# Reordering the end of the first mixture and moving the last additions to VectorE in a two-layer Perceiver kernel

## The chip, the cores and the metric

One Trainium2 chip, one core. The metric is the time of one execution on the device, in microseconds. The kernel is one launch with some 15,000 instructions on TensorE (matmuls), VectorE, ScalarE, GpSimd and SyncE (which issues most DMAs).

## The reference, cut to what matters

The input x is 8 sequences of 64 tokens by 256 features (512 tokens, four tiles of 128). A context of 8 x 1601 x 256 is read by cross-attention. Six steps run, each on a layer norm of x and added to x:

```python
x = x + L0_xattn(ln(x), ctx[:, :64]...)   # causal cross-attention, 16 heads of 16
x = x + L0_attn(ln(x))                    # attention through a latent of 64
x = x + L0_ffn(ln(x))                     # first mixture: 32 experts, top 4, and one shared
x = x + L1_xattn(ln(x), ctx)              # cross-attention on all 1601 keys
x = x + L1_attn(ln(x))                    # causal attention, inner layer norm
x = x + L1_ffn(ln(x))                     # second mixture: 8 experts, top 1, gelu
```

The layer norm is (x - mean) / sqrt(var + 1e-5) for each token. In the second mixture a token goes to one expert e and gets gelu(x W1[e] + b1[e]) W2[e] + b2[e].

## The kernel before, in words

Each engine runs one instruction list, written out by hand in the order in which it is issued; each engine is strictly in order, and semaphores join them. There is no planner. The tiles of x are x[:, t, :], t = 0 to 3, 128 tokens by 256 features in float32, kept in SBUF all the time.

**The end of the first mixture.** The 33 experts (L1626 up, L1640 down) add their outputs up in PSUM. For the last expert TensorE adds the four tiles in the order 0, 1, 2, 3 (L1682). Then TensorE issues 14 filler matmuls of 128x512 (keep_clock, L1315, called at L1687), which compute nothing that is used, and waits for the first normalized tile. VectorE meanwhile adds the sums to x: tile 0 (L1101), then measures tile 0 (bn_stats L881, bn_aggr L884), adds tile 1 (L1105) and tiles 2 and 3 at once (L1107), measures tiles 1 to 3 with the same two lines, and then scales tile 0 and tiles 1 to 3 (L892, called at L1110 and L1111). GpSimd computes the reciprocal root of the variance in two instructions (L446, L447), once for tile 0 and once for tiles 1 to 3.

From the normalized tile 0, TensorE makes two transposes (L1690), ScalarE copies them (L760), TensorE multiplies by the query weights (L1352), ScalarE scales and rounds the queries to bfloat16 (L766), and VectorE computes the remainders of that rounding (L1115, L1116, L1118), GpSimd copying some of them (L522, L524). TensorE then turns the queries (L1708, 16 transposes), ScalarE and VectorE copy them (L783, L1120), and the first scores (L1726) follow. Between the query product and L1708 stand TensorE's six transposes of tiles 1 to 3 (L1797), which wait for all of them to be normalized; ScalarE copies those in L781. On VectorE, L1115 is issued behind the scaling of tiles 1 to 3.

**The end of the second mixture.** Tokens are sorted into 11 blocks of 128 slots. Each block j goes through up (L1352), gelu (L866), down (L1948), and VectorE adds the bias into y_f (L1301). SyncE stores the first ten blocks to scratch_y in HBM in three DMAs (L378). Block 10 is not stored: TensorE sends it back to its tokens by a product with a one-hot matrix (L1971), one product for each tile of x, into PSUM banks. Once all three stores have landed, GpSimd issues four indirect DMAs (L558) that gather each token's row from scratch_y into y_back, tile by tile, and then adds each gathered tile to x (L564). VectorE adds the product of L1971 to that (L1308), tile by tile, and SyncE writes each tile to the output (L411).

Of the kernel before, what the change touches and what calls it, by code (L numbers as in the profile page):

```python
# [9 lines left out]
ALU = mybir.AluOpType  # L10
# [6 lines left out]
TT = TOK // P  # L17
# [21 lines left out]
NBLK = E1 + MORE  # L39
# [19 lines left out]
def build(nc, a, out, scratch_x, scratch_y, scratch_g):  # L59
    with ExitStack() as ctx:  # L60
        def sb(name, shape, dt=F32):
            return ctx.enter_context(nc.sbuf_tensor(name, shape, dt))

        def sem(name):
            return ctx.enter_context(nc.semaphore(name))
# [10 lines left out]
        x = sb("x", [P, TT, D])  # L76
        xn = sb("xn", [P, TT, D])
# [30 lines left out]
        def r2(n, dt=F32):  # L108
            at = used[0]
            used[0] += n  # L110
            assert used[0] <= 15344
            ap = R2[:, at:at + n]
            return ap if dt == F32 else ap.bitcast(dt)
# [77 lines left out]
        y_back = r2(TT * D).rearrange("p (t n) -> p t n", t=TT)  # L191
        ON_PE = (0, 1, NBLK - 1)
        oh = {j: r2(TT * P).rearrange("p (t s) -> p t s", t=TT) for j in ON_PE}
# [4 lines left out]
        def bank(i, n=512):  # L198
            return ps[:, i, 0:n]
# [9 lines left out]
        def w(key, at, n):  # L209
            o = W_COLS[key] + at  # L210
            return lambda c, lo=0, k=n: wall[:, c, o + lo:o + lo + k]
# [12 lines left out]
        def sems(prefix, names):  # L224
            return {n: sem(f"{prefix}_{n}") for n in names.split()}
# [59 lines left out]
        mq = sems("mq", "neg ln xt_ps xt q_ps qhi qf qs qdup qt_ps qt qt_b a_ps a_max nm row_ps row s_ps exp pv o o_ps y y_ps yt out_ps x")  # L285
        m0 = sems("m0", "x_hi x_lo log_ps sig mask pos_ps gate gt_ps gt sel up_a up_b silu t g r hi mid lo down end x gates_out")
        gb_in = [sem(f"gb_in{i}") for i in range(4)]
        w0_in = [sem(f"w0_in{i}") for i in range(4)]
        m1 = sems("m1", "zero zeroed log_ps mask count_ps pos_ps slot blocks oh sent h_ps act y_ps y added oht_ps oht fin out xg_ps xgt")
        w1_in = [sem(f"w1_in{i}") for i in range(WSLOTS)]  # L290
        w2_in = [sem(f"w2_in{i}") for i in range(WSLOTS)]
        bias_in = sem("bias_in")
# [2 lines left out]
        back = [sem(f"back{t}") for t in range(TT)]  # L295
# [120 lines left out]
        def _(pool):  # L416
# [125 lines left out]
            for k in range(4):  # L542
                t = 2 + k % 2
# [8 lines left out]
            for t in range(TT):  # L552
                pool.indirect_dma_start(
                    out=scratch_x[:, :], out_offset=bass.IndirectOffsetOnAxis(ap=f_si[:, t:t + 1], axis=0),
                    in_=xn[:, t, :], in_offset=None).then_inc(m1["sent"], 16)
            pool.wait_ge(stored, 16 * 3)
            for t in range(TT):
                pool.indirect_dma_start(  # L558
                    out=y_back[:, t, :], out_offset=None,
                    in_=scratch_y[:, :], in_offset=bass.IndirectOffsetOnAxis(ap=f_si[:, t:t + 1], axis=0)  # L560
                ).then_inc(back[t], 16)
            for t in range(TT):
                pool.wait_ge(back[t], 16)
                pool.tensor_tensor(x[:, t, :], x[:, t, :], y_back[:, t, :], ALU.add).then_inc(m1["added"], 1)  # L564


        @block.scalar
        def _(act):
# [303 lines left out]
        def _(dve):  # L872
            def lk(ins):
                link(dve, dve_chain, ins)
# [3 lines left out]
            def measure(src, lo_=0, hi_=TT):  # L878

                for t in range(lo_, hi_):  # L880
                    ins = dve.bn_stats(stats[:, t, :], src[:, t, :])  # L881
                lk(ins)
                for t in range(lo_, hi_):
                    ins = dve.bn_aggr(mv[:, t, :], stats[:, t, :])  # L884
                variances[0] += 1
                ins.then_inc(var_ready, 1)
                return variances[0]

            def scale(src, dst, done, n, lo_=0, hi_=TT):
                dve.wait_ge(rstd_ready, n)  # L890
                for t in range(lo_, hi_):
                    ins = dve.tensor_scalar(dst[:, t, :], src[:, t, :], mv[:, t, 0:1], rstd[:, t, :], ALU.subtract, ALU.mult)  # L892
                    if done is not None:
                        ins.then_inc(done, 1)
                if done is None:
                    lk(ins)
# [206 lines left out]
            first = measure(x, 0, 1)  # L1103
            dve.wait_ge(m0["end"], 2)
            dve.tensor_tensor(x[:, 1, :], sum0(1), x[:, 1, :], ALU.add).then_inc(m0["x"], 1)  # L1105
            dve.wait_ge(m0["end"], 3)
            dve.tensor_tensor(x[:, 2:4, :], bank(4).rearrange("p (t n) -> p t n", t=2), x[:, 2:4, :], ALU.add).then_inc(m0["x"], 2)  # L1107
            dve.wait_ge(m0["x"], TT)
            rest = measure(x, 1, TT)
            scale(x, xn, mq["ln"], first, 0, 1)  # L1110
            scale(x, xn, mq["ln"], rest, 1, TT)  # L1111
            Qg = Qs[:, 0:H, :].rearrange("p a (g d) -> p a g d", d=HD)
            q_ps = bank(7, D).rearrange("p (h d) -> p h d", h=H)
# [171 lines left out]
            def block_turned(j):  # L1285
                dve.wait_ge(m1["xg_ps"], j + 1)
                if j >= 2:
                    dve.wait_ge(m1["h_ps"], 2 * (j - 1))
                dve.tensor_copy(xgT[j % 2], bank(5 if j == 1 else 0, D).rearrange("p (c n) -> p c n", c=C)).then_inc(m1["xgt"], 1)  # L1289

            block_turned(0)
            block_turned(1)
            one_hot(NBLK - 1)
            dve.wait_ge(bias_in, 32)
            for j in range(NBLK):
                if j + 2 < NBLK:
                    block_turned(j + 2)
                if j == E1:
                    dve.wait_ge(more_bias_in, 32 * MORE)
                dve.wait_ge(m1["y_ps"], j + 1)  # L1300
                dve.tensor_tensor(y_f[:, j, :], bank(3 + j % 2, D), b2_s[:, j, :], ALU.add).then_inc(m1["y"], 1)  # L1301
                if j == 3:
                    dve.wait_ge(m1["oht_ps"], 1)
                    dve.tensor_copy(ohT, bank(5).rearrange("p (t s) -> p t s", t=TT)).then_inc(m1["oht"], 1)
            for t in range(TT):
                dve.wait_ge(m1["added"], t + 1)
                dve.wait_ge(m1["fin"], t + 1)
                dve.tensor_tensor(x[:, t, :], bank((0, 5, 6, 7)[t], D), x[:, t, :], ALU.add).then_inc(m1["out"], 1)  # L1308


        @block.tensor
        def _(pe):
            def keep_clock(n, at):
                for _ in range(n):
                    pe.matmul(bank(at), ident_b, mask_b, start=True, stop=True, skip_group_check=True)  # L1315
# [368 lines left out]
                    if k == 2 and t != 2:  # L1684
                        ins.then_inc(m0["end"], 1)
            wq, wo = w("1x", 0, D), w("1x", D + 32, D)
            keep_clock(14, 5)  # L1687
            pe.wait_ge(mq["ln"], 1)
            for c in range(C):
                ins = pe.transpose(ps[:, 6, c * P:(c + 1) * P], xn[:, 0, c * P:(c + 1) * P], ident)  # L1690
# [229 lines left out]
            def turn_block(j):  # L1920
                for i, (lo_, _) in enumerate(XG):
                    if j == lo_:
                        pe.wait_ge(xg_in[i], 16)
                if j >= 1:
                    pe.wait_ge(m1["xgt"], j)
                for c in range(C):
                    ins = pe.transpose(ps[:, 0, c * P:(c + 1) * P], xg[:, j, c * P:(c + 1) * P], ident)  # L1927
                ins.then_inc(m1["xg_ps"], 1)
# [115 lines left out]
```

## Time and profile before

| What | us |
|---|---|
| Median of three runs | 528.6 (528.46 to 528.76) |
| The profiled execution | 528.27 |
| Its span, first to last instruction | 526.4 |
| TensorE busy | 501.4 (95%) |
| VectorE busy | 324.5 (62%) |
| ScalarE busy | 299.7 (57%) |
| GpSimd busy | 124.3 (24%) |
| Granted TensorE clock, mean | 1.000 of full |

The span starts with the first instruction; all times below are counted from there. Busy time is summed for each engine and counts neither waits nor the issuing of DMAs. The 95% of TensorE is its busy share and includes filler matmuls. The profiled execution lies 0.33 us below the median of the runs.

### The profile page before, as it was taken

Reading aid. Unit: us, or ns where it says so; the run is one execution under the profiler, and the core shown is the slowest. Engines: PE = TensorE matmul, PEld = TensorE weight load, DVE = VectorE, ACT = ScalarE, POOL = GpSimd, SP = SyncE. Lnnn points to the kernel's source line nnn. Section 1 sums busy time; section 2 is a strip of 40 time slices with the busy share of each in tenths; the row PEclk is TensorE's granted clock in tenths of the full one; section 3 lists DMA queues with packets and bytes.
Section 4 is the critical chain, followed back from the end, with each engine's and each line's share of the span. In section 5 each row is a group of like instructions: output and inputs, shape, how many; then the busy total and the mean of one; then the engine's idle time right before and its main releaser. Section 6 shows DMA issues by size and latency. Waiting matters only on the chain.

```text
span 526.4 us, 15176 instructions
## 1 busy us (share of the span) xinstructions
PE 501.4 (95%) x6412; PEld 355.0 (67%) x6426; DVE 324.5 (62%) x672; ACT 299.7 (57%) x512; POOL 124.3 (24%) x218
## 2 busy tenths in 40 slices
PE   7999998899999999789999999999999989999996
PEld 4666676556666665455767767677567658999995
DVE  4652874666666666779899889999358674101101
ACT  2465485866656653477788877887734522233311
POOL 6124126733333333430000000000042033000005
PEclk9999999999999999999999999999999999999999
DMA  8977620135555552900000000000072002998813
GB/s 311 392 269 271 236 78 2 61 76 160 147 159 149 147 158 56 384 11 2 2 4 2 4 2 4 2 4 3 2 259 66 2 0 87 263 367 278 308 60 100
DMA packets 35346, 64.37 MB, mean 122 GB/s; under 512 B 3312, under 2 KB 25328, under 8 KB 34896
## 3 DMA queue, kind: packets, MB, share of 16 engines
q1 hardware_dynamic: 34752, 62.35, 35.9%
q8 instruction: 51, 0.84, 0.6%
q0 software_dynamic: 384, 1.05, 0.6%
q14 instruction: 15, 0.12, 0.1%
q10 hardware_dynamic: 144, 0.01, 0.0%
HBM read 59.40 MB, written 4.00 MB: 120 GB/s over the span
## 4 chain that ended last, share of the span: by engine, by line
PE 81%; DVE 7%; POOL 3%; ACT 3%; issue 2%; DMA 2%; SPq 0%; POOLq 0%; DVEq 0%; ACTq 0%
PE ps L1352 14%; PE ps L1626 10%; PE ps L1758 9%; PE ps L1726 9%; PE ps L1772 7%; PE ps L1640 7%; PE ps L1948 7%; PE ps L1471 2%; PE ps L1484 2%; PE ps L1458 2%; PE ps L1327 2%; PE ps L1435 1%; DVE region L1128 1%; DMA attn_weights<-in_wall 1%; PE ps L1377 1%
## 5 line engine op out<-in xcount | busy, mean ns | idle before, releaser
L1128 DVE TENSOR_REDUCE region<-ps 128x1 f32<-128x512 f32 x192 | 124.2, 687 | 16.2 <-PE ps L1726 16.1
L816 ACT ACTIVATE region<-ps 128x1024 f32<-128x1024 f32 (+1 forms) x112 | 106.0, 963 | 20.9 <-PE ps L1758 20.4
L1726 PE MATMUL ps<-ctx_kT,region 96*32 96x512 bf16 x768 | 82.0, 383 | 1.7 <-DVE region L1128 0.8
L1758 PE MATMUL ps<-region,ctx_kT 98*32 98x512 bf16 x832 | 72.5, 381 | 0.6 <-ACT region L794 0.4
L1772 PE MATMUL ps<-region,ctx_v 128*32 128x128 f32 (+1 forms) x1664 | 70.2, 272 | 0.0
L1626 PE MATMUL ps<-region 128*128 128x512 f16 x264 | 62.9, 379 | 1.0 <-ACT ctx_kT L589 0.7
L1772 PEld LDWEIGHTS ps<-region,ctx_v 128*32 128x32 f32 (+1 forms) x1664 | 56.7, 109 | 9.3 <-issue 0.3
L866 ACT ACTIVATE region<-ps,ctx_v 128x128 f32<-128x128 f32 x88 | 25.2, 368 | 59.7 <-PE ps L1352 59.7
L507 POOL TENSOR_TENSOR region<-region 128x512 f32<-128x512 f32 x33 | 38.2, 1156 | 64.2 <-ACT region L741 62.8
L1640 PE MATMUL ps<-region 128*128 128x256 bf16 x384 | 47.2, 273 | 0.9 <-DVE region L1075 0.9
L1640 PEld LDWEIGHTS ps<-region 128*128 128x128 bf16 x384 | 37.4, 98 | 12.4 <-DVE region L1075 1.7
L1626 PEld LDWEIGHTS ps<-region 128*128 128x128 bf16 x264 | 25.2, 98 | 25.8 <-ACT ctx_kT L589 0.8
L1083 DVE SCALAR_TENSOR_TENSOR region<-ps,region 128x512 f32<-128x512 f32 x33 | 22.8, 691 | 31.5 <-PE ps L1626 31.2
L1726 PEld LDWEIGHTS ps<-ctx_kT,region 96*32 96x32 bf16 x768 | 23.3, 94 | 26.5 <-DVE region L1128 15.2
L529 POOL CAST region<-region 128x4 bf16<-128x4 f32 x15 | 2.9, 190 | 135.6 <-DVE region L1138 135.6
L1352 PEld LDWEIGHTS ps<-region 128*128 128x128 f32 x288 | 33.3, 192 | 0.3
L1352 PE MATMUL ps<-region 128*128 128x128 f32 x288 | 33.4, 274 | 0.0
L735 ACT ACTIVATE region<-region 128x512 bf16<-128x512 f32 x33 | 20.8, 630 | 22.0 <-POOL region L507 22.0
L1758 PEld LDWEIGHTS ps<-region,ctx_kT 98*32 98x32 bf16 x832 | 25.1, 96 | 7.7 <-ACT region L794 1.3
L741 ACT ACTIVATE region<-region 128x512 bf16<-128x512 f32 x33 | 20.8, 629 | 15.8 <-DVE region L1096 15.6
L1301 DVE TENSOR_TENSOR region<-ps,ctx_v 128x256 f32<-128x256 f32 x11 | 4.7, 424 | 36.9 <-PE ps L1948 36.9
L1289 DVE COPY region<-ps 128x256 f32<-128x256 f32 x11 | 4.7, 425 | 34.4 <-PE ps L1927 33.0
(234 smaller groups left out, 821.5 us busy)
## 6 DMA issues: line engine op xcount, KB each, us to landing
region<-in_w SPq DMA_DIRECT2D x15, 1024.0 KB, 8.4
region<-in_ctxT SPq DMA_DIRECT2D x8, 1601.0 KB, 8.5
region<-gates SPq DMA_DIRECT2D x30, 256.0 KB, 3.4
ctx_kT<-in_w SPq DMA_DIRECT2D x7, 1024.0 KB, 7.3
region<-in_moe SPq DMA_DIRECT2D x33, 192.0 KB, 2.4
attn_weights<-in_wall SPq DMA_DIRECT2D x1, 2152.0 KB, 22.8
slots_x<-zeros SPq DMA_DIRECT2D x1, 1408.0 KB, 10.7
attn_weights<-in_wall SPq DMA_DIRECT2D x4, 256.0 KB, 5.8
```

The lines of the kernel that those rows point to most:

```text
L507: pool.tensor_tensor(hr[n % 2], t2[n % 2], hp[n % 4][0], ALU.subtract).then_inc(m0["r"], 1)
L816: act.activation(probs[u % NP_][:, 0:512 * n_keys], ps[:, pr:pr + n_keys, :].rearrange("p b n -> p (b n)"), ACT.Exp).then_inc(mq["exp"], 1)
L866: ins = act.activation(hT[j % 2][:, k, :], ps[:, (1, 6)[j % 2] + hh, (k % 4) * P:(k % 4 + 1) * P], ACT.Gelu, bias=b1_s[:, j, k:k + 1])
L1083: ins = dve.scalar_tensor_tensor(out=dst, in0=bank(n % 2), scalar=1.0 / XS, in1=sa[n % 2], op0=ALU.mult, op1=ALU.mult)
L1128: ins = dve.tensor_reduce(mp[g % 2][:, j // 3, j % 3:j % 3 + 1], bank(4 + n % 2), AX.X, ALU.max)
L1352: ins = pe.matmul(dst, lhs(c), rhs(c), start=(c == 0), stop=(c == C - 1))
L1626: ins = pe.matmul(bank(n % 2 if part else 2 + n % 2), wn[:, c * 256 + part * 128:c * 256 + part * 128 + 128], xp[k][:, c, :], start=(c == ...
L1640: ins = pe.matmul(sum0(t), hp[n % 4][k][:, t * P:(t + 1) * P], w0[n % 4][:, 512:768], start=(n == 0 and k == 0 and t < 3), stop=False, ski ...
L1726: ins = pe.matmul(ps[32 * i:32 * i + 32, at, :], QT[0:KQ, b, h + i // 2, 32 * (i % 2):32 * (i % 2) + 32], kT[0:KQ, b, 512 * c:512 * c + 51 ...
L1758: ins = pe.matmul(ps[32 * c:32 * c + 32, 2 * (u % 2) + i, :], kT[0:KQ2, b, k * P + 32 * c:k * P + 32 * c + 32], QT[0:KQ2, b, 8 * r:8 * r + ...
L1772: ins = pe.matmul(ps[32 * c:32 * c + 32, 7, 0:P], v_ctx[0:rows_, b, k, :], probs[u % NP_][0:rows_, 512 * i + P * c:512 * i + P * (c + 1)], ...
L1948: ins = pe.matmul(bank(3 + j % 2, D), hT[j % 2][:, k, :], w2_s[j % WSLOTS][:, k, :], start=(k == 0), stop=(k == HC - 1))
```

## The change

At the end of the first mixture, VectorE scales tile 0 right after the additions, ahead of measuring tiles 1 to 3, and TensorE issues 10 filler matmuls instead of 14. At the end of the second mixture, GpSimd adds nothing any more: VectorE adds the gathered tiles 0 and 1 before the y addition of the last block, tile 2 before the first output addition, and tile 3 between the second and the third. Each of them waits for its own gather, and VectorE waits for each (lk) before its next instruction. The semaphore "added" goes.

```diff
-            for t in range(TT):
-                pool.wait_ge(back[t], 16)
-                pool.tensor_tensor(x[:, t, :], x[:, t, :], y_back[:, t, :], ALU.add).then_inc(m1["added"], 1)
...
             dve.tensor_tensor(x[:, 2:4, :], bank(4).rearrange("p (t n) -> p t n", t=2), x[:, 2:4, :], ALU.add).then_inc(m0["x"], 2)
+            scale(x, xn, mq["ln"], first, 0, 1)
             dve.wait_ge(m0["x"], TT)
             rest = measure(x, 1, TT)
-            scale(x, xn, mq["ln"], first, 0, 1)
             scale(x, xn, mq["ln"], rest, 1, TT)
...
+            def add_gathered(t):
+                dve.wait_ge(back[t], 16)
+                lk(dve.tensor_tensor(x[:, t, :], x[:, t, :], y_back[:, t, :], ALU.add))
...
+                if j == NBLK - 1:
+                    add_gathered(0)
+                    add_gathered(1)
                 dve.wait_ge(m1["y_ps"], j + 1)
                 dve.tensor_tensor(y_f[:, j, :], bank(3 + j % 2, D), b2_s[:, j, :], ALU.add).then_inc(m1["y"], 1)
...
-            for t in range(TT):
-                dve.wait_ge(m1["added"], t + 1)
+
+            def add_last(t):
                 dve.wait_ge(m1["fin"], t + 1)
                 dve.tensor_tensor(x[:, t, :], bank((0, 5, 6, 7)[t], D), x[:, t, :], ALU.add).then_inc(m1["out"], 1)
+
+            add_gathered(2)
+            add_last(0)
+            add_last(1)
+            add_gathered(3)
+            add_last(2)
+            add_last(3)
...
-            keep_clock(14, 5)
+            keep_clock(10, 5)
             pe.wait_ge(mq["ln"], 1)
```

## Rows read from the trace of the kernel before

**Rows 1.** The chain that ended last, shares of the span by engine.
```profile
PE 81%; DVE 7%; POOL 3%; ACT 3%; issue 2%; DMA 2%; SPq 0%; POOLq 0%; DVEq 0%; ACTq 0%
```

**Rows 2.** Timeline, 208.6 to 217 us: start, length, engine, line, operation, count.
```profile
208.62 2.97 PE L1315 MATMUL ps<-const_bf 128*128 128x512 bf16 x13
...
209.60 0.68 DVE L1107 TENSOR_TENSOR x<-ps,x 128x512 f32<-128x512 f32 x1
...
209.78 0.58 POOL L447 TENSOR_TENSOR ln_rstd<-ln_rstd,const_f 128x1 f32<-128x1 f32 x1
...
210.31 1.08 DVE L881 BATCH_NORM_STATS2 ln_stats<-x 128x6 f32<-128x256 f32 x3
...
211.66 0.38 DVE L892 TENSOR_SCALAR xn<-x,ln_mean_var,ln_rstd 128x256 f32<-128x256 f32 x1
...
212.09 0.44 PE L1690 MATMUL ps<-const_f,xn 128*128 128x128 f32 x2 [0.51 <-DVE xn L892]
...
213.01 1.13 PE L1352 MATMUL ps<-attn_weights,xnT 128*128 128x256 f32 x4 [0.47 <-ACT xnT L760]
213.14 1.06 DVE L892 TENSOR_SCALAR xn<-x,ln_mean_var,ln_rstd 128x256 f32<-128x256 f32 x3 [1.10 <-POOL ln_rstd L447]
214.18 0.38 ACT L766 ACTIVATE region<-ps 128x256 bf16<-128x256 f32 x1 [1.22 <-PE ps L1352]
...
214.25 0.88 PE L1797 MATMUL ps<-const_f,xn 128*128 128x128 f32 x6
...
214.59 0.42 DVE L1115 SCALAR_TENSOR_TENSOR region<-ps,region 128x256 bf16<-128x256 f32 x1 [0.39 <-ACT region L766]
...
214.91 0.85 ACT L781 ACTIVATE xnT<-ps 128x384 f32<-128x384 f32 x2
...
215.38 0.42 DVE L1118 TENSOR_TENSOR region<-region 128x256 bf16<-128x256 f32 x1
...
215.86 1.09 PE L1708 MATMUL ps<-const_bf,region 128*96 128x128 bf16 x16 [0.73 <-DVE region L1118]
...
216.54 0.59 ACT L783 ACTIVATE region<-ps 96x512 bf16<-96x512 bf16 x1 [0.78 <-PE ps L1708]
```

**Rows 3.** Timeline of TensorE in the first 9 us.
```profile
1.31 3.59 PE L1510 MATMUL ps<-yT 128*128 128x512 bf16 x8 [1.31 <-POOL yT L471]
...
8.73 0.51 PE L1435 MATMUL ps<-attn_weights,ctx64T 128*64 128x128 f32 x5 [1.17 <-DMA attn_weights<-in_wall]
```

**Rows 4.** Timeline, 516 to 524.4 us.
```profile
516.24 0.98 POOL L558 DMA_INDIRECT region<-slots_y,region  x1 [73.48 <-DMA slots_y<-region]
...
520.03 0.95 POOL L558 DMA_INDIRECT region<-slots_y,region  x1 [0.30 <-issue]
520.42 0.42 DVE L1301 TENSOR_TENSOR region<-ps,ctx_v 128x256 f32<-128x256 f32 x1 [6.60 <-PE ps L1948]
...
520.90 2.00 PE L1971 MATMUL ps<-region 128*128 128x256 f32 x8 [0.52 <-DVE region L1301]
521.00 2.77 POOL L564 TENSOR_TENSOR x<-x,region 128x256 f32<-128x256 f32 x4
...
522.23 2.37 SPq L411 DMA_DIRECT2D out<-x  x4
...
523.80 0.42 DVE L1308 TENSOR_TENSOR x<-ps,x 128x256 f32<-128x256 f32 x1 [0.25 <-POOL x L564]
```

**Rows 5.** The four gathers of L558, from issue to landing.
```profile
DMA to landing us min/median/max: 2.7/2.8/2.8
```

**Rows 6.** L1060 and L553: durations min/median/max in ns.
```profile
L1060 DVE TENSOR_TENSOR region<-const_f,region x3: 327/328/643, 102.2 to 103.9; 128x128 f32<-128x128 f32 x3
...
L553 POOL DMA_INDIRECT slots_x<-xn,region x4: 960/1005/1354, 437.5 to 441.7; - x4
```

**Rows 7.** Busy times, clock, DMA share and GB/s while one output tile moves.
```profile
523.00:523.70 0.70, 0.00 (x0) 0.00 (x0) 0.42 (x1) 0.00 (x0) 0.70 (x2) 1.00 0.55 187
```

More of the change, by code:

```diff
@@ L288, in build @@
         w0_in = [sem(f"w0_in{i}") for i in range(4)]
-        m1 = sems("m1", "zero zeroed log_ps mask count_ps pos_ps slot blocks oh sent h_ps act y_ps y added oht_ps oht fin out xg_ps xgt")
+        m1 = sems("m1", "zero zeroed log_ps mask count_ps pos_ps slot blocks oh sent h_ps act y_ps y oht_ps oht fin out xg_ps xgt")
         w1_in = [sem(f"w1_in{i}") for i in range(WSLOTS)]
```

## The prediction

> **What bounds the kernel now.** I read the chain of waits on the page first. It is TensorE for 81% of the span, with VectorE at 7% and GpSimd at 3% [rows 1]. The reader is to see that an edit on VectorE or GpSimd counts only where TensorE stands still. The change touches two such places: the hand-over from the first mixture to the cross-attention (208 to 217 us) and the last 8 us. Everything between is only shifted by what the first place gives. So I read the timeline of both places [rows 2, 4] and ask at each which arrival comes last.
>
> **Part 1, the first mixture's end.** Now the two remaining additions end at 210.28 (209.60 + 0.68, L1107). The root of tile 0 is ready at 210.36 (209.78 + 0.58, L447), while VectorE measures tiles 1 to 3 from 210.31 and scales tile 0 only at 211.66 [rows 2]. After the change the scaling waits for the later of the two, 210.36, plus 0.03 (the pause between L1107 and L881 in rows 2). So it starts at 210.39, 1.27 us earlier, and ends at 210.77 (0.38).
>
> What follows for tile 0: the transposes (L1690) at 210.83 instead of 212.09; the query product (L1352) 0.92 later, as now, at 211.75 instead of 213.01; its end at 212.88; ScalarE's copy (L766) done at 213.30 instead of 214.56 [rows 2].
>
> What follows for tiles 1 to 3: their measuring starts behind the scaling. Neighbouring VectorE instructions overlap by some 0.05 us (three of L881 take 1.08), so it starts at 210.72 instead of 210.31, 0.41 late. The aggregation, GpSimd's root and the scaling x3 follow one upon another, so the scaling x3 runs at 213.55 to 214.61 instead of 213.14 to 214.20, and the six transposes (L1797) at 214.66 instead of 214.25, done at 215.54 [rows 2].
>
> Here is the point on which this part hangs. The next step of tile 0's chain, L1115 on VectorE, needs L766, but it is queued behind the scaling of tiles 1 to 3. Now it waits for L766 (starts 214.59, VectorE idle since 214.20) [rows 2]. Afterwards L766 is ready 1.29 us before VectorE is free. L1115 starts at 214.53 to 214.62, depending on whether it overlaps the scaling or not: a change of -0.06 to +0.03, and I take -0.06, since L881 and L892 x3 in the same rows overlap. L1118 and the query transposes L1708 (215.86 now) shift by as much. Beside it, the six transposes end before 215.80; ScalarE's L781 ends at 215.76 + 0.41 = 216.17, before L783 is wanted at 216.48 [rows 2]. The 1.27 us bought for tile 0 is therefore lost in VectorE's queue, and the 0.41 us lost for the rest falls into the 0.39 us that VectorE waited there.
>
> The ten filler matmuls instead of 14 (13 recorded in 2.97, 0.23 each) end near 210.7 instead of 211.59, just before the transposes at 210.83: no delay from them, and none removed, since TensorE already stood idle before 212.09. But TensorE now has nothing from 212.88 to 214.66, 1.78 us, where it had 0.11 (213.01 + 1.13 to 214.25). That is the first rival.
>
> **Part 2, the end of the kernel.** The four gathers start from 516.24 to 520.03, 1.26 apart, and land 2.8 us after their start [rows 4, 5]: at 519.0, 520.3, 521.6 and 522.8. GpSimd adds them only once it has issued all four: 521.00 to 523.77, 0.69 each, and the last output addition (L1308) at 523.80 follows the last of these [rows 4].
>
> The price of one such addition on VectorE: no row shows it with these operands. From below 0.33 us (L1060, 128x128, two SBUF operands) [rows 6], from above 0.68 us (L1107, twice as wide) [rows 2]; I take 0.42, the 128x256 of L1118 [rows 2].
>
> - Additions 0 and 1 sit ahead of the last block's y addition (L1301, 520.42 now). Addition 0 runs at 519.03, in idle time. Addition 1 waits for 520.3 and runs until 520.72, and each is awaited before the next instruction. So the y addition starts near 520.80, 0.38 late. Queued behind it is TensorE's last group L1971 (four products in 2.00 us), which ends at 523.28 instead of 522.90.
> - Addition 2: 521.6 to 522.02. Output additions 0 and 1: 522.10 and 522.45, both products there (the first by about 522.0, the next 0.43 later).
> - Addition 3: 522.83 (landing) to 523.25. Output addition 2: about 523.33. Output addition 3: 523.67, its product there since 523.28, so 0.39 of slack. It ends at 524.09 instead of 524.22.
>
> VectorE's end moves by -0.13. With 0.33 an addition it would be -0.22, with 0.68 it would be +0.13. The last two output DMAs now follow each other by 0.34 instead of 0.68 [rows 4]. A 0.7 us stretch that holds one of them keeps the DMA engines 55% busy [rows 7], 0.39 us of full work, so the last can queue up to about 0.08 behind its neighbour. I take -0.05 for the part, with bounds -0.22 and +0.21.
>
> Do the additions disturb the gathers? GpSimd is generating gather 2 (518.8 to 519.7) during addition 0 and gather 3 (from 520.03) during addition 1. A VectorE addition of two SBUF operands took 643 ns instead of 327 beside GpSimd work, and an indirect DMA beside a VectorE burst took 1354 ns instead of 1005 [rows 6]. So both directions can cost: third rival.
>
> By the Trainium skill, page "SBUF — State Buffer", section "Who interferes with whom", a VectorE instruction with two SBUF inputs contends with a GpSimd instruction that reads SBUF, and the second to come is fully blocked; the same section infers that a tensor_tensor leaves descriptor generation alone, which would make it zero here. The trace shows the first for L1060, and nothing in it shows the second.
>
> **The sum.** 528.27 (the profiled execution; its span is 526.4) - 0.06 - 0.05 = 528.16. The runs' median, 528.6, lies 0.33 above that execution, so I forecast 528.5 us. Its own range is 528.2 to 528.8 by the bounds above (-0.28 to +0.24), widened by 0.1. About 0.2% (1.06 us) can be told from no change, so below 527.5 is faster and above 529.7 slower.
>
> **The rivals.**
> - Low clock (slower). After the 1.78 us without a matmul, the granted clock falls from 2.4 to 1.2 GHz. Against: it stayed at full over 1.17 us of nothing at 7.56 us [rows 3]. For: 1.17 us is the longest gap between matmuls in the trace before its last microseconds, so 1.78 us lies outside what it shows. Price: at the start of the kernel eight 128x512 matmuls took 3.59 us, 0.45 each, against 0.23 for the fillers [rows 2, 3]; that stretch was at least 3.6 us long, and I take 4. Four such microseconds from 215.9 on, where TensorE sets the pace, do the work of two: +2.0, 530.5 us. If it falls only for the idle time, it costs nothing. Chance 0.12.
> - The whole gain passes (faster). Tile 0's queries come 1.27 us earlier through to the first scores: 527.2 us. It would need L1115 ahead of the scaling of tiles 1 to 3 in VectorE's order, which it isn't. I leave 0.06 for this and for any other shift of the schedule over 1 us.
> - Additions and gathers disturb each other. If addition 1 is held until gather 3 is issued (520.98), the y addition is 1.05 late, L1971 ends at 523.95 and the output at 524.4: +0.18 in place of -0.13, 528.8. If instead the gathers stretch by 0.35 each (1354 - 1005), the last lands 0.7 later: 529.2. Both stay within what counts as no change. Chance 0.10.
> - The tail doesn't move since the span's end hangs on something else: 528.55, the same answer, inside the forecast.
>
> **How the numbers follow.** Forecast 0.72, clock 0.12, whole gain 0.06, disturbance 0.10. Of the forecast's share I give 0.02 to each side for what I have not seen, so faster 0.08, same 0.78, slower 0.14. The range 527.9 to 529.6 holds forecast and disturbance and leaves out the two ends, less than 2 in 10.
>
> **What would show it.** L892 for tile 0 at 210.4; the x3 scaling at 213.55; L1115 directly behind it with no wait for ScalarE; L1708 within 0.1 of 215.86; the granted clock 1.00 through 212 to 222. At the end: the y addition at 520.8, L1971 0.38 later, the last output addition at 523.7 and waiting for the gather, not for GpSimd. Wrong if L1708 moves by more than 0.3 us, if matmuls after 215 take twice their time, or if the gathers start more than 1.3 us apart.

## The result, and the profile after

| | Kernel before | Changed kernel |
|---|---|---|
| Median, 20 executions each | 528.6 us | 529.26 us |
| Range | 528.07 to 529.69 | 528.75 to 532.74 |
| Mean granted clock | 1.000 in the profiled execution | 0.990 to 0.997 in 19 executions, 1.000 in one (528.91 us) |

The ratio is 1.0018 with a 95% interval of 1.001 to 1.0025: slightly slower, where I forecast slightly faster. The time lies inside the range that I gave, but on the other side of 528.6, and the experiments below lay this to the granted clock. The profiled execution is the slowest of the 20 (532.74 us). 2.56 us of that are not the change's: the first addition of the stage, L1097 here, starts at 210.84 against 208.27, behind an unchanged first mixture. Three waits of TensorE for DMAs account for about that much: 2.46 us instead of 1.17 for the attention weights at 9.6 us, and 0.63 and 0.73 us for the experts' weights at 120.44 and 145.63, where the trace of the kernel before has no such wait of 0.5 us or more. Over the 12 profiles of the experiments, all with the same first mixture, that start lies between 208.4 and 210.0. So from here on I count within the two changed places from that addition ("from the stage's start"), and at the end from the first gather.

The share of the span by engine in the chain that ended last, for the changed kernel (compare [rows 1]):

```profile
PE 65%; issue 16%; DVE 7%; POOL 4%; DMA 4%; ACT 3%; SPq 0%; POOLq 0%; DVEq 0%; ACTq 0%
```

The timeline of the changed kernel around the end of the first mixture (start, length, engine, line, operation; it answers to [rows 2], whose lines 1315, 892, 881, 1690, 1352, 1115, 1797, 1118, 1708 are 1325, 888, 877, 1700, 1362, 1111, 1807, 1114, 1718 here):

```profile
210.84 0.43 DVE L1097 TENSOR_TENSOR x<-ps,x 128x256 f32<-128x256 f32 x1 [0.38 <-PE ps L1692]
...
210.96 2.32 PE L1325 MATMUL ps<-const_bf 128*128 128x512 bf16 x10
...
212.96 0.41 DVE L888 TENSOR_SCALAR xn<-x,ln_mean_var,ln_rstd 128x256 f32<-128x256 f32 x1
213.29 1.07 DVE L877 BATCH_NORM_STATS2 ln_stats<-x 128x6 f32<-128x256 f32 x3
...
213.42 0.44 PE L1700 MATMUL ps<-const_f,xn 128*128 128x128 f32 x2
...
214.34 1.13 PE L1362 MATMUL ps<-attn_weights,xnT 128*128 128x256 f32 x4 [0.47 <-ACT xnT L756]
...
216.04 1.11 DVE L888 TENSOR_SCALAR xn<-x,ln_mean_var,ln_rstd 128x256 f32<-128x256 f32 x3 [1.33 <-POOL ln_rstd L447]
217.07 0.41 DVE L1111 SCALAR_TENSOR_TENSOR region<-ps,region 128x256 bf16<-128x256 f32 x1
...
217.20 1.54 PE L1807 MATMUL ps<-const_f,xn 128*128 128x128 f32 x6 [1.74 <-DVE xn L888]
...
217.85 0.42 DVE L1114 TENSOR_TENSOR region<-region 128x256 bf16<-128x256 f32 x1
...
218.54 1.91 PE L1718 MATMUL ps<-const_bf,region 128*96 128x128 bf16 x16
```

Read it against [rows 2]. L1111 starts with no wait of its own, right behind the scaling x3. TensorE waits 1.74 us ahead of L1807 (the gap foreseen as 1.78). Then the same six transposes take 1.54 us instead of 0.88, and the sixteen of L1718 take 1.91 instead of 1.09. The busy times in four stretches give the reason (PE, PEld, DVE, ACT, POOL busy, then the granted clock, DMA share and GB/s):

```profile
211.00:216.30 5.30, 3.85 (x18) 1.73 (x15) 3.75 (x13) 1.15 (x3) 2.23 (x5) 1.00 0.78 252
216.40:219.80 3.40, 2.60 (x18) 2.59 (x19) 2.00 (x7) 1.15 (x3) 0.40 (x1) 0.50 1.08 382
219.80:223.20 3.40, 3.40 (x19) 1.75 (x17) 1.54 (x3) 1.45 (x2) 0.00 (x0) 0.50 1.06 372
223.20:226.60 3.40, 3.40 (x29) 1.75 (x28) 2.51 (x4) 1.32 (x4) 2.29 (x5) 1.00 1.03 377
```

The granted clock is at 0.50, that is 1.2 of 2.4 GHz, from 216.4 to 223.2 us: it fell inside the gap from 215.47 (214.34 + 1.13) to 217.20.

The end of the kernel (L1289 is the addition of a gathered tile, L1304 the y addition, L1981 the last products, L1311 the output addition; compare [rows 4]):

```profile
520.89 0.99 POOL L558 DMA_INDIRECT region<-slots_y,region  x1 [73.55 <-DMA slots_y<-region]
...
523.44 0.95 POOL L558 DMA_INDIRECT region<-slots_y,region  x1 [0.30 <-issue]
523.65 0.43 DVE L1289 TENSOR_TENSOR x<-x,region 128x256 f32<-128x256 f32 x1 [5.19 <-DMA region<-slots_y,region]
524.70 0.95 POOL L558 DMA_INDIRECT region<-slots_y,region  x1 [0.31 <-issue]
524.95 0.43 DVE L1289 TENSOR_TENSOR x<-x,region 128x256 f32<-128x256 f32 x1 [0.87 <-DMA region<-slots_y,region]
525.41 0.42 DVE L1304 TENSOR_TENSOR region<-ps,ctx_v 128x256 f32<-128x256 f32 x1
...
525.89 2.00 PE L1981 MATMUL ps<-region 128*128 128x256 f32 x8 [0.87 <-DVE region L1304]
526.20 0.43 DVE L1289 TENSOR_TENSOR x<-x,region 128x256 f32<-128x256 f32 x1 [0.36 <-DMA region<-slots_y,region]
526.70 0.79 DVE L1311 TENSOR_TENSOR x<-ps,x 128x256 f32<-128x256 f32 x2
...
527.42 0.42 DVE L1289 TENSOR_TENSOR x<-x,region 128x256 f32<-128x256 f32 x1
527.88 0.76 DVE L1311 TENSOR_TENSOR x<-ps,x 128x256 f32<-128x256 f32 x2
```

The output is complete on VectorE 7.75 us after the first gather started (528.64 - 520.89), against 7.98 before (524.22 - 516.24). On VectorE the tail is 0.23 us faster, and the y addition's 0.34 us delay (4.52 against 4.18 after the first gather) is hidden.

### The profile page after: what moved, and what is told of

Its sections match the earlier page's. It is cut to its first block, busy times and chain, and to the rows that moved or that the text cites. A ratio compares the mean times of both kernels' runs of the same rounds, so it can differ in the third digit from the quotient of the medians.

```text
span 530.9 us, 15182 instructions
## 1 busy us (share of the span) xinstructions
PE 504.6 (95%) x6422; PEld 356.3 (67%) x6422; DVE 326.2 (61%) x676; ACT 300.1 (57%) x512; POOL 121.5 (23%) x214
## 3 DMA queue, kind: packets, MB, share of 16 engines
q0 software_dynamic: 384, 1.05, 0.6%
## 4 chain that ended last, share of the span: by engine, by line
PE 65%; issue 16%; DVE 7%; POOL 4%; DMA 4%; ACT 3%; SPq 0%; POOLq 0%; DVEq 0%; ACTq 0%
PE ps L1636 9%; PE ps L1768 9%; PE ps L1736 9%; PE ps L1782 7%; PE ps L1650 7%; PE ps L1362 7%; PE ps L1494 2%; PE ps L1481 2%; PE ps L1468 2%; PE ps L1337 2%; DMA region<-in_moe 2%; PE ps L1445 1%; DVE region L1124 1%; DMA attn_weights<-in_wall 1%; PE ps L1387 1%
## 5 line engine op out<-in xcount | busy, mean ns | idle before, releaser
L1362 PEld LDWEIGHTS ps<-region 128*128 128x128 f32 x288 | 33.3, 192 | 0.3
L1362 PE MATMUL ps<-region 128*128 128x128 f32 x288 | 33.5, 274 | 0.0
L927 DVE TENSOR_REDUCE region<-ps 128x8 f32<-128x512 f32 x24 | 16.5, 689 | 14.2 <-PE ps L1468 13.9
```

What stands on the lines that cost most here:

```text
L1362: ins = pe.matmul(dst, lhs(c), rhs(c), start=(c == 0), stop=(c == C - 1))
```

## The experiments

Theory: the clock's fall in the new gap makes the change slower; without it the change is worth some -0.1 to -0.2 us. Rival: the moved additions cost it at the end. Each kernel ran 12 times, beside 35 runs of the kernel before on the same chip; three chips served the three groups. "Low" are executions whose mean granted clock was 0.997 or less, and medians are given apart for the two kinds. The kernel before's own executions are counted without a single one of 537.83 us.

| Kernel | Median us | Low | Median, full clock | Median, low | Ratio to before (95%) |
|---|---|---|---|---|---|
| *first group: before* | 528.83 | 9 of 34 | 528.48 | 529.69 | |
| after_fill14 | 529.17 | 6 of 12 | 528.00 | 529.73 | 0.9998 (0.9984 to 1.0013) |
| after_gapfill | 528.66 | 2 of 12 | 528.58 | 529.76 | 0.9992 (0.9976 to 1.0008) |
| before_fill10 | 529.94 | 9 of 12 | 528.26 | 530.08 | 1.0010 (0.9996 to 1.0025) |
| tail_only | 528.52 | 4 of 12 | 528.39 | 530.15 | 0.9997 (0.9982 to 1.0012) |
| *second group: before* | 529.35 | 13 of 35 | 528.94 | 530.02 | |
| after_again | 529.45 | 8 of 12 | 528.40 | 529.71 | 0.9998 (0.9983 to 1.0012) |
| head_only | 529.10 | 6 of 12 | 528.45 | 529.44 | 0.9998 (0.9985 to 1.0011) |
| reordered | 529.40 | 4 of 12 | 529.03 | 530.56 | 1.0005 (0.9990 to 1.0020) |
| reordered_route | 528.63 | 0 of 12 | 528.63 | | 0.9988 (0.9975 to 1.0000) |
| *third group: before* | 529.23 | 10 of 35 | 528.87 | 530.17 | |
| before_route | 528.90 | 0 of 12 | 528.90 | | 0.9995 (0.9980 to 1.0009) |
| after_route | 530.05 | 12 of 12 | | 530.05 | 1.0016 (1.0000 to 1.0033) |
| gapfill_route | 528.37 | 0 of 12 | 528.37 | | 0.9990 (0.9975 to 1.0005) |
| fill14_route | 528.21 | 0 of 12 | 528.21 | | 0.9982 (0.9967 to 0.9998) |

**First group: which part is it?**

```diff
 after_fill14 (on the changed kernel)
-            keep_clock(10, 5)
+            keep_clock(14, 5)
```

> The changed kernel with 14 fillers again instead of 10 at the end of the first mixture. Clock theory (the change is slower because TensorE's granted clock falls to half for some 3.5 us in the gap behind the first query product, and the rest of the change is worth about -0.1 us): the fillers now end near 211.6 on the scale of the kernel before, the first transposes wait for them and not for VectorE (0.8 us later than with 10), the gap behind the query product shrinks from 1.8 to about 1.0 us, the clock stays at 1.000, and the time is the kernel before's -0.1 (within 0.3). Rival, the tail (VectorE's four additions disturb gathers or hold the y addition): the clock is 1.000 and the time stays 0.6 to 1.0 us above the kernel before.

The first transposes did wait for the fillers (3.15 us from the stage's start, against 2.58 with 10), and this cost the query transposes only 0.02 us (7.50 against 7.48 in after_again). But the clock was low in 6 of 12 and the time 529.17 beside 528.83, both against my expectation. The profiled execution shows where: not at the first mixture's end, but in the routing of the second mixture, which the change doesn't touch.

```profile
431.80:435.20 3.40, 2.52 (x28) 1.63 (x28) 1.81 (x15) 1.85 (x3) 0.00 (x0) 1.00 0.00 0
435.20:438.70 3.50, 3.50 (x14) 1.53 (x11) 3.31 (x16) 0.00 (x0) 0.75 (x1) 0.51 0.02 5
```

So there are two places, and every count until then mixed them. That the kernel before had low executions as well (9 of 34) was new too: its one profile had shown 1.000 throughout.

```diff
 after_gapfill (on the changed kernel)
             queries(0)
+            keep_clock(7, 5)
             pe.wait_ge(mq["ln"], TT)
```

> The changed kernel, 10 fillers kept, and 7 more fillers of 128x512 behind the first query product (1.6 us in the 1.8 us gap). Clock theory: clock 1.000, nothing delayed since TensorE stood idle there, time the kernel before's -0.1 (within 0.3), 0.6 to 1.0 below the changed kernel. Tail rival: as slow as the changed kernel, +0.6 to +1.0.

Two low executions of 12 instead of 19 of 20. The median is 528.66, 0.17 below the kernel before's beside it, in the expected direction but within its interval. Where the two low ones fell isn't shown.

```diff
 before_fill10 (on the kernel before)
-            keep_clock(14, 5)
+            keep_clock(10, 5)
```

> The kernel before with only the fillers cut from 14 to 10; VectorE's order and the tail as before. TensorE is then idle 1.4 us ahead of the first transposes, 0.5 ahead of the query product, 0.1 and 0.7 behind it: as much in sum (2.7 us) as in the changed kernel (2.6 us), but no single gap of 1.8. If the fall of the clock hangs on the sum of idle time over these 5 us, the clock falls here too (0.997 or so) and the time is +0.4 to +1.0. If it hangs on the one long gap, the clock is 1.000 and the time is the kernel before's within 0.2.

The clock fell in 9 of 12, beside 9 of 34 for the kernel before, with VectorE's order untouched: cutting four fillers alone is enough, and no single gap of 1.74 us is needed. The longest here is 1.38 us, and the fall, at 214.8, came after it, while TensorE worked on the query product. Some of the nine may be falls in the routing, as in after_fill14; the profiled one is not. Its timeline on TensorE, and the clock from 214.9 on:

```profile
213.05 0.44 PE L1690 MATMUL ps<-const_f,xn 128*128 128x128 f32 x2 [1.38 <-DVE xn L892]
213.96 1.27 PE L1352 MATMUL ps<-attn_weights,xnT 128*128 128x256 f32 x4 [0.47 <-ACT xnT L760]
215.21 1.54 PE L1797 MATMUL ps<-const_f,xn 128*128 128x128 f32 x6
```
```profile
214.90:218.20 3.30, 3.10 (x19) 2.39 (x19) 1.55 (x5) 1.91 (x5) 0.80 (x2) 0.50 1.08 384
```

```diff
 tail_only (on the kernel before: the change's last part alone)
-                pool.tensor_tensor(x[:, t, :], x[:, t, :], y_back[:, t, :], ALU.add).then_inc(m1["added"], 1)
...
+                lk(dve.tensor_tensor(x[:, t, :], x[:, t, :], y_back[:, t, :], ALU.add))
```

> The kernel before with only the last part of the change: VectorE instead of GpSimd adds the gathered rows. Clock theory: clock 1.000, the last output addition starts at 523.65 to 523.7 instead of 523.80 and the time is -0.05 to -0.15. Tail rival: +0.6 to +1.0, with gathers further apart than 1.3 us or a y addition over 0.5 us late.

As expected and against the rival: 528.52, and 528.39 where the clock is full, beside 528.48. The gathers start 1.25 to 1.30 us apart, against 1.24 to 1.28 before. The interval still reaches +0.6 us, so it is the trace that clears the tail: VectorE ends 7.82 us after the first gather, against 7.98. With that, only the head is left.

**Second group: the change again, its head alone, and the lost 1.27 us.**

after_again is the changed kernel, unaltered.

> The changed kernel once more, unaltered, beside the three others. Clock theory: the granted clock falls in nearly every execution (mean 0.996 or 0.997) and the time is +0.4 to +1.0 on the kernel before. Rival (its first measurement was a chip's or a run's peculiarity): clock 1.000 in most executions and a time within 0.2 of the kernel before.

Inconclusive for the time: 8 of 12 low against 13 of 35, ratio 0.9998. With some 1.2 us for a low execution (next section), 67% against 37% makes +0.36, and with -0.2 for the rest of the change +0.2: less than 12 executions resolve. Its profiled execution had the full clock.

```diff
 head_only (on the kernel before)
             dve.tensor_tensor(x[:, 2:4, :], ...)
+            scale(x, xn, mq["ln"], first, 0, 1)
             dve.wait_ge(m0["x"], TT)
             rest = measure(x, 1, TT)
-            scale(x, xn, mq["ln"], first, 0, 1)
...
-            keep_clock(14, 5)
+            keep_clock(10, 5)
```

> Only the first part of the change: VectorE scales tile 0 first, 10 fillers; the tail as before. Clock theory: falls in nearly every execution, +0.5 to +1.1. Tail rival: no slower than the kernel before. Either way L1708's counterpart starts 7.48 us after the first addition of the stage when the clock is full (7.59 in the kernel before).

6 of 12 low, where nearly all were expected; the profiled one fell in the head:

```profile
212.70:216.10 3.40, 1.42 (x12) 0.90 (x11) 2.20 (x6) 1.59 (x4) 1.57 (x3) 1.00 1.10 378
216.20:219.60 3.40, 3.40 (x25) 2.24 (x23) 1.71 (x3) 1.61 (x2) 0.00 (x0) 0.50 1.05 394
```

The query transposes started 7.48 us from the stage's start, just as foretold, since the clock fell only at 7.8: 1.5 us behind the end of the 1.74 us gap, with TensorE at work since 214.72 but for a wait of 0.25. The time (529.10 beside 529.35) is a miss for the clock theory's +0.5 to +1.1.

```diff
 reordered (on after_gapfill)
 VectorE:
-            scale(x, xn, mq["ln"], rest, 1, TT)
             (L1111, L1112, L1114: remainders of tile 0's queries)
+            scale(x, xn, mq["ln"], rest, 1, TT)
 TensorE:
             keep_clock(7, 5)
+            turn_queries(0, 0, 2)
+            turn_queries(0, 1, 3)
             pe.wait_ge(mq["ln"], TT)
 (ScalarE copies the turned queries ahead of tiles 1 to 3 as well.)
```

> The changed kernel with three further edits: VectorE computes the remainders of tile 0's queries ahead of scaling tiles 1 to 3, TensorE turns tile 0's queries ahead of transposing tiles 1 to 3 (and ScalarE copies in that order), and 7 fillers stand in the gap behind the first query product. If tile 0's 1.27 us are lost in VectorE's queue, as predicted, they now come through: the query transposes start about 6.3 us after the stage's first addition instead of 7.5, the first scores 1.0 to 1.3 us earlier, and the time is 0.8 to 1.3 us below the kernel before where the clock stays full. Rival: the first scores are held by something else (tiles 1 to 3, now 1.0 us later, are wanted by the second query product), and the time is the kernel before's -0.2 to +0.2.

The query transposes came at 6.35 us from the stage's start instead of 7.48, and the first scores at 8.13 instead of 8.81. Then nothing was left of it. TensorE in reordered, and then in gapfill_route, whose head is that of after_gapfill (stage's starts 210.02 and 208.43):

```profile
217.34 0.88 PE L1810 MATMUL ps<-const_f,xn 128*128 128x128 f32 x6
218.15 0.62 PE L1736 MATMUL ps<-ctx_kT,region 96*32 96x512 bf16 x8
219.37 1.13 PE L1362 MATMUL ps<-attn_weights,xnT 128*128 128x256 f32 x4 [0.61 <-ACT xnT L781]
```
```profile
214.79 0.87 PE L1808 MATMUL ps<-const_f,xn 128*128 128x128 f32 x6 [0.22 <-DVE xn L888]
...
217.24 0.62 PE L1736 MATMUL ps<-ctx_kT,region 96*32 96x512 bf16 x8 [0.24 <-ACT region L779]
217.79 1.13 PE L1362 MATMUL ps<-attn_weights,xnT 128*128 128x256 f32 x4
```

The second query product (L1362) starts 9.35 us from the stage's start in the one and 9.36 in the other. In reordered it waits 0.61 us for ScalarE's copy of tiles 1 to 3, which were pushed back. The rival written down with it holds: tiles 1 to 3 bound the stage from the second query product on.

```diff
 reordered_route (on reordered)
             positions(1)
-            keep_clock(2, 7)
+            keep_clock(5, 7)
             pe.wait_ge(m1["mask"], 2)
```

> The same with three more fillers (5 instead of 2) in the routing of the second mixture, where TensorE waits 0.8 us for VectorE's mask. The kernel before and the others show a mean clock of 0.996 in a quarter of their executions; if those falls sit in the routing, as one trace showed (435.2 to 438.6 us), they become rarer here than in the kernel without these three, and the median is 0.2 to 0.4 us lower. If they come from elsewhere, as many executions show 0.996 as before.

No low execution in 12, where reordered had 4. The median is 0.77 lower than reordered's, more than the 0.2 to 0.4 expected; between two kernels of 12 executions each, spread over 2 to 3 us, that excess is not resolved.

**Third group: both places apart.** All four have the three fillers of the last diff in the routing: on the kernel before (before_route), on the changed kernel (after_route), on after_gapfill (gapfill_route) and on after_fill14 (fill14_route).

> The kernel before with three more fillers in the routing of the second mixture (5 instead of 2), its head and tail untouched. If the kernel before's own executions with a clock of 0.996 (22 of 69 so far) fall in the routing, none or one of 12 shows it here and the median is 0.2 to 0.4 us below the kernel before. If they fall at the first mixture's end, 3 to 5 of 12 show it still.

> The changed kernel with the same three fillers and nothing in the gap behind the first query product. Clock theory with the place at the first mixture's end: half or more of the 12 executions still show 0.996 or 0.997, in the profile near 216 us, and they are 0.5 to 1.3 us slower than the full ones. If all falls sat in the routing, none shows here and the time is 0.2 to 0.4 below the kernel before.

> The changed kernel with both places filled (7 fillers behind the first query product, 3 more in the routing). Clock 1.000 in at least 11 of 12. Its distance to before_route, whose clock should be as full, is the worth of the change without the clock: -0.2 us by the traces (-0.1 at the first scores, -0.1 at the end). That is below what 5 rounds resolve; in the trace the first scores start 8.81 us after the stage's first addition against 8.91.

> The changed kernel with 14 fillers ahead of the first transposes, as in the kernel before, and the three in the routing. By the sum-of-idle theory it is clean (0 or 1 of 12 falls), since TensorE is idle 1.8 us over the stage instead of 2.6; the six falls of 12 seen with 14 fillers sat in the routing. If 3 or more fall, some still sit at the first mixture's end, by the 1.25 us gap that is left there. Time where the clock is full: as gapfill_route.

0, 12, 0 and 0 of 12. With the routing filled, the kernel before never falls and the changed kernel always does. Seven fillers in the gap or the four restored ahead of the first transposes each end it. TensorE in after_route, and its clock:

```profile
215.49 1.54 PE L1807 MATMUL ps<-const_f,xn 128*128 128x128 f32 x6 [1.73 <-DVE xn L888]
216.82 1.90 PE L1718 MATMUL ps<-const_bf,region 128*96 128x128 bf16 x16
```
```profile
211.80:215.10 3.30, 1.48 (x6) 0.79 (x6) 1.94 (x9) 1.18 (x3) 1.48 (x3) 1.00 1.03 396
215.20:218.50 3.30, 3.01 (x22) 3.00 (x22) 1.74 (x5) 1.56 (x3) 0.40 (x1) 0.50 1.08 387
```

And fill14_route, where a gap of 1.25 us stays and the same transposes take 0.87 and 1.09:

```profile
213.12 1.13 PE L1362 MATMUL ps<-attn_weights,xnT 128*128 128x256 f32 x4 [0.47 <-ACT xnT L756]
215.51 0.87 PE L1807 MATMUL ps<-const_f,xn 128*128 128x128 f32 x6 [1.25 <-DVE xn L888]
216.63 1.09 PE L1718 MATMUL ps<-const_bf,region 128*96 128x128 bf16 x16 [0.25 <-DVE region L1114]
```

after_route is 1.15 us above before_route (530.05 - 528.90) and 1.68 above gapfill_route, all on one chip; after_route and gapfill_route differ in nothing but the seven fillers. fill14_route, the changed kernel with its fillers back and three more in the routing, has the lowest median of all: 528.21 beside 529.23, ratio 0.9982 (0.9967 to 0.9998). It isn't told apart from gapfill_route (528.37).

## Why the prediction was wrong

**The step that failed** is the chance of 0.12 for "Low clock", set because "it stayed at full over 1.17 us of nothing at 7.56 us". I weighed one gap against the longest other gap. The runs show that this is no measure: before_fill10 falls in 9 of 12 with no gap over 1.38 us, and fill14_route never with one of 1.25. The changed kernel's own profiled execution says the same from the other side: near its start TensorE waited 2.46 us for a DMA, and the granted clock reads 1.00 there and after it.

```profile
9.60 1.97 PE L1445 MATMUL ps<-attn_weights,ctx64T 128*64 128x128 f32 x32 [2.46 <-DMA attn_weights<-in_wall]
```

The term that I put at nothing is the cut of four fillers: "no delay from them, and none removed", since TensorE stood idle there anyway. Their cover was not time but clock. With 10 and the routing filled, 12 of 12 executions are low; with 14, none.

**Its price** was the other error. I wrote +2.0 us for four microseconds at half clock. In four traces the fall lasted 3.4 us, in one twice that, and its cost depends on when it comes. (The rows that I priced it from don't show a fall: the eight matmuls of 0.45 us at 1.31 to 4.90 us stand where the granted clock is recorded as 1.00. That matmuls take nearly twice their time at 0.50 is shown by L1807, 1.54 us against 0.87.) Take the distance from the stage's start to the first gather, which is 307.83 to 308.01 us in the nine traces at full clock. before_fill10, fallen 5.6 us from the stage's start, has 308.58: 0.63 lost against before_route (307.95). after_route, fallen at 6.0, has 308.63: 0.76 lost against gapfill_route (307.87). head_only, fallen at 7.8 when TensorE was busy for all of the 3.4 us, has 309.15: 1.23 against after_again (307.92). In the profiled execution of the change the clock stayed low twice as long, and the distance is 310.05: 2.13. The fall in the routing in after_fill14 cost 1.11 (309.02 against 307.91 in fill14_route). By executions, a low clock goes with 1.08 to 1.30 us more in the kernel before's three groups. So the chance of 0.12 met 19 low executions of 20, and the price was 1.6 to 3 times too high.

**The sum by these numbers.** In the first measurement 19 of 20 executions of the changed kernel were low. Over the three groups the kernel before was low in 32 of 104. So it carries about 0.31 x 1.2 = 0.37 us of falls, and the changed kernel 0.95 times 0.6 to 1.2, that is 0.6 to 1.1 us. With -0.2 for the rest of the change the sum is 0.0 to +0.5, and measured were +0.66 in the medians, +0.5 to +1.3 by the interval. The two meet only at the edge: more than one fall in an execution would add to it, but one fall of 3.4 us in 528 makes a mean of 0.997, and only two of the 20 lie clearly lower (0.993 and 0.990, with 532.74 and 531.94 us). So part of the +0.66 may be left without a cause. The sum also rests on the kernel before's share on other chips, since its clock in its first 20 executions isn't recorded one by one.

**Part 1, VectorE's queue: right.** Predicted -0.06 us at the query transposes; measured at full clock (after_again) 7.48 against 7.59 from the stage's start, -0.11, and the first scores 8.81 against 8.92. The stage's start and the first scores of the kernel before, then the same and the query transposes of after_again:

```profile
208.27 0.42 DVE L1101 TENSOR_TENSOR x<-ps,x 128x256 f32<-128x256 f32 x1 [0.38 <-PE ps L1682]
...
217.19 0.61 PE L1726 MATMUL ps<-ctx_kT,region 96*32 96x512 bf16 x8 [0.24 <-ACT region L783]
```
```profile
208.38 0.43 DVE L1097 TENSOR_TENSOR x<-ps,x 128x256 f32<-128x256 f32 x1 [0.38 <-PE ps L1692]
...
215.86 1.09 PE L1718 MATMUL ps<-const_bf,region 128*96 128x128 bf16 x16 [0.25 <-DVE region L1114]
...
217.19 0.61 PE L1736 MATMUL ps<-ctx_kT,region 96*32 96x512 bf16 x8 [0.24 <-ACT region L779]
```

By the distance to the first gather the new order is worth as much: 307.83 to 307.93 in the six traces that have it, 307.95 to 308.01 in the three that don't. L1111 starts with no wait, directly behind the scaling. The 1.27 us for tile 0 were lost there as said; but "The whole gain passes" needed more than I wrote, since reordered gave tile 0 its way and the second query product took it back.

**Part 2, the tail: right in mechanism and order of size.** An addition took 0.43 us (I took 0.42), the y addition came 0.34 late (0.38), the last products ended 0.34 later and had slack. VectorE's end moved by -0.23 instead of -0.13: the last gathered addition began 0.06 earlier than I had it (6.53 us after the first gather, against 6.59), and the three instructions behind each other followed more closely than I allowed. At the span's end less is left of it. The span ends 10.0 to 10.1 us after the first gather in the ten traces with the new tail and 10.1 to 10.2 in the four with the old, some 0.05 apart in the mean, as the -0.05 supposed with its queueing of the last output DMA. The two ends of the price, 0.33 and 0.68, did not matter.

**Slips in the working.** By its own bounds (528.6, +0.24, and 0.1 on top) the forecast's range ends at 528.9, not 528.8. The queueing of the last DMA comes to 0.05 by its rows (0.39 - 0.34), where 0.08 is written. The overlap taken as 0.05 between L892 and L881 was 0.08 (213.37 to 213.29). None of them moves the answer.

**Disturbance between additions and gathers: not there.** Two of the additions lie inside a gather's generation on GpSimd (523.65 in 523.44 to 524.39, and 524.95 in 524.70 to 525.65); the additions took 0.43, as the ones alone, and the gathers 0.95, as the last two before. The row that the rival rested on was weaker than I read it: of the three L1060, the two at 0.33 us (103.22, 103.94) ran beside GpSimd copies as well, and only the one at 102.18, beside a GpSimd tensor_tensor, took 0.64. By the Trainium skill, "SBUF — State Buffer", section "Who interferes with whom", a two-input VectorE instruction contends with GpSimd's reads, but is inferred to leave descriptor generation alone. The trace bears out that second half; the first, read as covering the indirect DMA, would have held the y addition 1.05 us.

**Open.** What sets off a fall in one execution and not in the next, with the same instructions, isn't shown: the changed kernel was low in 19 of 20, in 8 of 12 and, with the routing filled, in 12 of 12, and its head alone in 6 of 12 on the chip of the 8. Only the profiled executions show where a fall came. Whether the chips differ isn't shown either, nor where the difference in time of the first measurement went in after_again (ratio 0.9998). That the routing holds the kernel before's falls rests on 0 of 12 with three fillers more, and on one trace of after_fill14; no profile of the kernel before itself caught one. And gapfill_route and fill14_route lie 0.53 and 0.69 us below before_route, all at full clock, where the traces account for about 0.1; with 12 executions each, spread over 1.6 to 1.9 us, the rest is not resolved.

## What to carry to other kernels

A filler matmul in idle time costs little to keep (14 instead of 10 cost the query transposes 0.02 us) and can be dear to drop: 0.6 to 1.2 us here for one fall. When an edit moves work so that TensorE's waits are shared out anew, judge the whole stretch and not the longest gap, and look at the granted clock of every execution, since one profile at 1.000 hid a fall in three of ten. In an in-order queue, ask first what stands ahead of the next link of the chain that you speed up.

## What the runs showed of the hardware that I had not expected

The granted clock of an unchanged kernel fell in 32 of 104 executions, and those took 1.08 to 1.30 us more of 528. Three filler matmuls of 128x512, 0.23 us each, in a wait of 0.8 us went with a full clock in all 48 executions of the four kernels that had them in the routing and a filled head (before_route, gapfill_route, fill14_route, reordered_route), while the stage ahead of them could still be low in 12 of 12 (after_route). A fall lasted 3.4 us and in one trace twice as long. It came in the gap itself (after, after_route) or while TensorE was at work behind it (before_fill10, head_only), and a wait of 2.46 us near the kernel's start brought none.
